# Joint stage with the sums by src four steps ahead and four-step loops, bonds ahead of rows in the sort, and a count of dst ids by comparisons in groups of twelve

## The reference

```python
# layer 0
feat_in  = x @ W_in.T + b_in;  feat_out = x @ W_out.T + b_out
a_in  = seg_mean(feat_in[src],  dst, N)      # edges grouped by dst
a_out = seg_mean(feat_out[dst], src, N)      # edges grouped by src
x = layernorm(x + gru(concat(a_in, a_out), x))
# layer 1
m = relu(concat(x[src], x[dst], bond) @ W1 + b1) @ W2 + b2
m = m * sigmoid(bond @ Wa + ba)
x = layernorm(x + (x + segment_sum(m, src, N)))
```

## Time and profile before

| | |
|---|---|
| median of three runs | 13780.42 us (13775.32 to 13793.6) |
| profiled execution | 13790.1 us, its span 13788.4 us |
| count of dst ids (`load_constants_and_count`) | 0 to 125 us |
| tables and id lists | 125 to 232 us |
| `sum_in_first` | 232 to 2343 us |
| `sort_records` | 2343 to 6660 us |
| joint stage (`sum_rest`) | 6661 to 8841 us |
| node update, messages, finish | 8841 to 13788 us |
| busy shares of the span | PE 63%, DVE 61%, ACT 20%, POOL 70% |

### The profile page before, as it was taken

How to read it: one execution, slowest core, us unless ns; L and a number is a source line. 1 busy time by engine, 2 the same in 40 slices (tenths; PEclk the granted TensorE clock), 3 DMA queues, 4 the chain that set the end, 5 groups by cost and what they waited for, 6 DMA issues and landing times. The chain is left out here.

```text
span 13788.4 us, 248865 instructions
## 1 busy us (share of the span) xinstructions
PE 8650.6 (63%) x53687; PEld 7661.1 (56%) x53688; DVE 8351.6 (61%) x29389; ACT 2713.3 (20%) x7251; POOL 9705.6 (70%) x10125
## 2 busy tenths in 40 slices
PE   3777776333333333333577777797888888888876
PEld 2555554333333333333577777556777777777775
DVE  6555555666666666666677777554444455444444
ACT  0000000111111111111000000154444444444444
POOL 3777776777777777777777777306777777777774
PEclk9555555555656555666788888898999999999998
DMA  5822223666666666666677777513333334333336
GB/s 178 308 54 54 54 54 84 197 198 196 199 196 199 197 199 196 199 196 199 174 187 186 186 186 186 95 52 76 80 79 79 80 88 94 80 79 80 79 79 82
DMA packets 2665496, 1884.08 MB, mean 137 GB/s; under 512 B 1375795, under 2 KB 2460371, under 8 KB 2664784
## 3 DMA queue, kind: packets, MB, share of 16 engines
q1 hardware_dynamic: 1505269, 806.75, 22.1%
q0 software_dynamic: 377360, 782.89, 19.9%
q10 hardware_dynamic: 782662, 292.60, 8.8%
HBM read 1509.53 MB, written 483.44 MB: 145 GB/s over the span
## 5 line engine op out<-in xcount | busy, mean ns | idle before, releaser
L1846 POOL DMA_INDIRECT p<-q_rows,small x3432 | 3250.1, 947 | 1643.5 <-issue 1000.0
L1051 PE MATMUL bank<-p,ring 128*128 x6656 | 1549.0, 426 | 2714.7 <-DVE ring L972 2711.5
L1051 PEld LDWEIGHTS bank<-p,ring 128*128 128x128 f32 x6656 | 1437.8, 328 | 2826.1 <-issue 2826.1
L1110 POOL DMA_INDIRECT edges_a<-ring,small x1664 | 1635.7, 983 | 563.1 <-issue 441.4
L1110 POOL DMA_INDIRECT edges_b<-ring,small x1664 | 1632.5, 981 | 507.6 <-issue 441.1
L799 POOL DMA_INDIRECT ring<-in_x,ring x1664 | 1573.9, 946 | 533.7 <-issue 530.0
L1884 PE MATMUL bank<-ring 128*128 128x256 f32 x3432 | 1205.4, 437 | 766.4 <-DVE p L1796 766.1
L830 PE MATMUL bank<-ring 128*128 128x129 f32 x3328 | 1240.3, 491 | 617.8 <-DMA ring<-in_x,ring 525.1
L1252 POOL DMA_INDIRECT ring<-in_x,small x1352 | 1278.7, 946 | 463.2 <-issue 411.3
L1272 PE MATMUL bank<-p,ring 128*128 128x129 f32 x8360 | 1194.3, 312 | 525.1 <-DVE ring L1200 525.1
L1272 PEld LDWEIGHTS bank<-p,ring 128*128 128x128 f32 x8360 | 1157.7, 226 | 562.5 <-issue 562.5
(11 more groups left out here) (289 smaller groups left out, 14195.4 us busy)
## 6 DMA issues: line engine op xcount, KB each, us to landing
p<-rows_by_slot SPq DMA_DIRECT2D x418, 928.0 KB
p<-edges_b SPq DMA_DIRECT2D x530, 262.0 KB
p<-edges_a SPq DMA_DIRECT2D x520, 262.0 KB
bonds_by_dst<-in_bond ACTq DMA_DIRECT2D x5, 20625.0 KB, 159.1
ring<-edges_a ACTq DMA_DIRECT2D x1792, 33.0 KB
p<-q_rows,small POOLq DMA_INDIRECT x3432
ring<-edges_b ACTq DMA_DIRECT2D x1664, 33.0 KB
ring<-bonds_by_dst ACTq DMA_DIRECT2D x1672, 32.0 KB
```

The lines of the kernel that those rows point to most:

```text
L1051: last = nc.tensor.matmul(found[q][:, j, :], hot_t[g % GRPS][:, QUAD * h + j, :], x, start=True, stop=True, skip_group_check=True)
L1110: pool.indirect_dma_start(out=c.edges[s], out_offset=bass.IndirectOffsetOnAxis(ap=pos[:, k:k + 1], axis=0), in_=rec[:, k, :], in_offset=No ...
L1846: pool.indirect_dma_start(out=gath[g][:, k, :], out_offset=None, in_=c.q_dram, in_offset=bass.IndirectOffsetOnAxis(ap=gidx[g][:, k:k + 1], ...
```

## The change

**Joint stage.** `ids` is split into two transfers: `load_ids` brings the gather indices alone, `load_locals` (new, ring of four) the local numbers. SyncE's pass v becomes: windows of v; wait until `s_hot_in` (counts of `prepare_in`, started at 3) is at least v; locals of v; wait for the last gather of step v-3; ids of v+5. The work by src runs four steps ahead of that by dst: VectorE's turn u is `add_in(u)`, `add_out(u+4)`, `prepare_out(u+6)` in halves, `prepare_in(u+2)`, and TensorE's is `sum_in(u)`, `sum_out(u+5)`; before the loops VectorE does `add_out` and `prepare_out` of four steps, and TensorE `sum_out` of five. The block numbers are read in two register loads, eight before `add_in` and five before `add_out`. The loops of VectorE and TensorE hold four steps instead of eight; the last two loop turns (eight steps) are written out without loop, and leave out what lies past the last step. `sum_out` is zeroed by ScalarE instead of VectorE, which waits for it before its first `add_out`; GpSimd waits for no zeroing.

**Sort.** In SyncE's loop the wait for scatters and the load of bonds stand ahead of the wait for comparisons and the load of rows.

**Count.** Two shifts over all 3300 ids on VectorE, two copies to bf16 on ScalarE, ahead of its weight loads; then five batches of 660 ids. Each batch is 13 + 8 comparisons of 660 bf16 digits with a constant, one for each digit value, into one-hots laid out in groups of twelve ids (group, digit, id); TensorE sums 55 products a batch, now 96 x 156 outputs. The order check is one comparison, written as bf16, ahead of the batches, and its sum is made by ten products with ones on TensorE. Everything is written out without loop.

```diff
-HC, CG = 110, 5
+HC, CG = 660, 12
...
 # ScalarE, ahead of its weight loads
+            for k in range(2):
+                act.wait_ge(s_digit, k + 1)
+                nc.scalar.copy(digits[k], whole[k]).then_inc(s_cast, 1)
...
+            nc.vector.tensor_scalar(whole[0], raw[:, 1, 0:TT], 10, None, ALU.logical_shift_right).then_inc(s_digit, 1)
+            nc.vector.tensor_scalar(whole[1], raw[:, 1, 0:TT], 7, 7, ALU.logical_shift_right,
+                                    ALU.bitwise_and).then_inc(s_digit, 1)
...
-            with dve.Fori(0, HSTEPS // 2) as i:
-                step.loop(i, 4)
-                for n in range(2):
-                    ids = raw[:, 1, bass.ds((2 * i + n) * HC, HC)]
-                    dve.wait_ge(s_cnt, 2 * i + n)
-                    step.mark(nc.vector.tensor_scalar(digits[0], ids, 10, None, ALU.logical_shift_right))
-                    step.link(nc.vector.tensor_scalar(digits[1], ids, 7, 7, ALU.logical_shift_right, ALU.bitwise_and))
-                    for dig, hot, width in ((digits[0], us[n], HU), (digits[1], vs[n], HV)):
-                        nc.vector.tensor_tensor(
-                            hot, dig.unsqueeze(2).to_broadcast([TP, HC, width]),
-                            c.iota[0:TP, 0:width].unsqueeze(1).to_broadcast([TP, HC, width]),
-                            ALU.is_equal).then_inc(s_dig, 1)
...
+            nc.vector.tensor_tensor(after, raw[:, 1, 0:TT], raw[:, 1, 1:TT + 1], ALU.is_gt).then_inc(s_viol, 1)
+            dve.wait_ge(s_cast, 2)
+            for i in range(HSTEPS):
+                n = i % 2
+                if i >= 2:
+                    dve.wait_ge(s_cnt, i - 1)
+                for dig, hot, width in ((digits[0], us[n], HU), (digits[1], vs[n], HV)):
+                    for d in range(width):
+                        nc.vector.tensor_scalar(hot[:, :, d, :], dig[:, i * HC:(i + 1) * HC].rearrange("p (g t) -> p g t", t=CG),
+                                                float(d), None, ALU.is_equal).then_inc(s_dig, 1)
...
-            step.link(nc.vector.tensor_tensor(after[:, 0:TT], raw[:, 1, 0:TT], raw[:, 1, 1:TT + 1], ALU.is_gt))
-            nc.vector.reduce_sum(viol, after[:, 0:TT], AXX).then_inc(s_viol, 1)
...
 # TensorE
+            for i in range(HSTEPS):
+                n = i % 2
+                pe.wait_ge(s_dig, (HU + HV) * (i + 1))
+                for t in range(APART):
+                    last = nc.tensor.matmul(cross, vs[n][:, t, :, :].rearrange("p d t -> p (d t)"),
+                                            us[n][:, t, :, :].rearrange("p d t -> p (d t)"),
+                                            start=(i == 0 and t == 0), stop=(i == HSTEPS - 1 and t == APART - 1))
+                last.then_inc(s_cnt, 1)
+            pe.wait_ge(s_viol, 1)
+            for t in range(0, TT, HC // 2):
+                last = nc.tensor.matmul(c.bank[2][0:1, 0:HC // 2], c.ones[0:TP, 0:1], after[:, t:t + HC // 2],
+                                        start=(t == 0), stop=(t == TT - HC // 2))
...
 # sort_records, SyncE
+                        sp.wait_ge(s_sc[2 * (g % GRPS)], i * (2 * QUAD * 16) + g // GRPS * (QUAD * 16))
+                        load_bonds(u, 2 * (g % GRPS))
                         sp.wait_ge(s_hot, u * 4 + 12)
                         load_rows(u + 2, g % 2)
-                        sp.wait_ge(s_sc[2 * (g % GRPS)], i * (2 * QUAD * 16) + g // GRPS * (QUAD * 16))
-                        load_bonds(u, 2 * (g % GRPS))
...
 # sum_rest, SyncE
+            def load_locals(u, n):
+                sp.dma_start(local[n], c.slots_d[:, bass.ds(u + B_GROUP, 1), LOCAL * HALF:(LOCAL + 1) * HALF]
+                             .rearrange("p o w -> p (o w)")).then_inc(s_loc[n], 16)
...
-                        u = i * LOOK + g
-                        load_windows(u, g % 2, edges)
-                        sp.wait_ge(s_agg_in, u * NI + (IN_0 - (LOOK - AHEAD - 1) * NI))
-                        load_ids(u + AHEAD, (g + AHEAD) % LOOK)
-            for k in range(2):
-                load_windows(QSTEPS + k, k, c.edges[1])
+                        v, last = i * LOOK + g, (g - 3) % GRPS * HALF + HALF - 1
+                        load_windows(v, g % 2, edges)
+                        sp.wait_ge(s_hot_in, v)
+                        load_locals(v, g % TURN_V)
+                        sp.wait_ge(s_g[last], i * (16 * LOOK // GRPS) + 16 * ((g - 3) // GRPS + 1))
+                        load_ids(v + AHEAD, (g + AHEAD) % LOOK)
...
 # VectorE; HOT_0 = 3, LEAD = TURN_V = 4
+            dve.sem_inc(s_hot_in, HOT_0)
-            nc.vector.memset(c.sum_out, 0.0).then_inc(s_zero, 1)
...
+            def turn(i, g, most=QSTEPS):
+                u = i * TURN_V + g
+                add_in(u, blocks_in(u))
+                if g + LEAD < most:
+                    add_out(u + LEAD, g, blocks_out(u + LEAD))
+                for h in range(NO):
+                    if g + LEAD + 2 < most:
+                        prepare_out(i, (g + LEAD + 2) % TURN_V, h, (g + LEAD + 2) // TURN_V)
+                if g + 2 < most:
+                    prepare_in(i, (g + 2) % TURN_V, (g + 2) // TURN_V)
...
+            dve.wait_ge(s_blank, 1)
+            for v in range(LEAD):
+                add_out(v, v, blocks_out(v))
+                for h in range(NO):
+                    prepare_out(0, (v + 2) % TURN_V, h, (v + 2) // TURN_V)
+            with dve.Fori(0, TURNS_S - 2) as i:
+                step.loop(i, TURN_V * NO)
+                for g in range(TURN_V):
+                    turn(i, g)
...
+            nc.scalar.activation(c.sum_out.rearrange("p b d -> p (b d)"),
+                                 c.ones_f[:, 0:1].to_broadcast([P, (NB + 1) * W]), ACT.Copy, scale=0.0).then_inc(s_blank, 1)
...
-            sum_out(0, 0)
-            with pe.Fori(0, QSTEPS // LOOK) as i:
-                for g in range(LOOK):
 # TensorE
+            for v in range(LEAD + 1):
+                sum_out(v, v)
+            with pe.Fori(0, TURNS_S - 2) as i:
+                for g in range(TURN_V):
                     sum_in(i, g)
-                    sum_out(i * LOOK + (g + 1), (g + 1) % LOOK)
+                    sum_out(i * TURN_V + (g + LEAD + 1), g + LEAD + 1)
```

More of the change, by code:

```diff
@@ L226, in load_constants_and_count @@
     pairs = c.pairs()
-    after = scratch[:, 7000:7000 + TT // 2].bitcast(BF16)
-    digits = [scratch[:, 9000 + 200 * n:9000 + 200 * n + HC].bitcast(I32) for n in range(2)]
-    us = [scratch[:, 9600 + 750 * n:9600 + 750 * n + HC * HU // 2].bitcast(BF16).rearrange("p (t d) -> p t d", d=HU)
-          for n in range(2)]
-    vs = [scratch[:, 11200 + 500 * n:11200 + 500 * n + HC * HV // 2].bitcast(BF16).rearrange("p (t d) -> p t d", d=HV)
-          for n in range(2)]
+    after = c.blk_s[0:TP, 0:TT]
+    digits = [scratch[:, 6610 + k * (TT // 2):6610 + (k + 1) * (TT // 2)].bitcast(BF16) for k in range(2)]
+    top = 6610 + TT
+    whole = [scratch[:, top + k * TT:top + (k + 1) * TT].bitcast(I32) for k in range(2)]
+    us = [scratch[:, top + n * (HC * HU // 2):top + (n + 1) * (HC * HU // 2)].bitcast(BF16)
+          .rearrange("p (g d t) -> p g d t", d=HU, t=CG) for n in range(2)]
+    vs = [at.bitcast(BF16).rearrange("p (g d t) -> p g d t", d=HV, t=CG)
+          for at in (c.part(7200, HC * HV // 2)[0:TP, :], c.tab[0:TP, 0:HC * HV // 2])]
+    assert top + HC * HU <= (NB + 1) * XW and 7200 + HC * HV // 2 <= RINGW and HC * HV // 2 <= S_COLS
     spare = 2 * TT
@@ L326, in _ @@
-            step.end(HSTEPS // 2)
+            dve.wait_ge(s_edge, 16)
+            nc.vector.tensor_tensor(after, raw[:, 1, 0:TT], raw[:, 1, 1:TT + 1], ALU.is_gt).then_inc(s_viol, 1)
[8 more added lines that the diff above has]
+                                                float(d), None, ALU.is_equal).then_inc(s_dig, 1)
@@ L340, in _ @@
         def _(pe):
-            pe.sem_inc(s_cnt, 1)
             pe.wait_ge(s_z, 8)
-            nc.tensor.matmul(cross, zero16[:, 0:1].to_broadcast([TP, CG * HU]),
-                             zero16[:, 0:1].to_broadcast([TP, CG * HV]), start=True, stop=False)
-            with pe.Fori(0, HSTEPS // 2) as i:
-                for n in range(2):
-                    pe.wait_ge(s_dig, 4 * i + 2 * n + 2)
-                    for t in range(0, HC, CG):
-                        last = nc.tensor.matmul(cross, us[n][:, t:t + CG, :].rearrange("p t d -> p (t d)"),
-                                                vs[n][:, t:t + CG, :].rearrange("p t d -> p (t d)"),
-                                                start=False, stop=False)
-                    last.then_inc(s_cnt, 1)
@@ L1141, in sum_rest @@
     lo_out = c.small[:, 24:24 + QPS * QW]
-    ids = [c.small[:, 128 + n * 2 * HALF:128 + (n + 1) * 2 * HALF].rearrange("p (f k) -> p f k", k=HALF) for n in range(LOOK)]
+    ids = [c.small[:, 128 + n * HALF:128 + (n + 1) * HALF] for n in range(LOOK)]
+    local = [c.small[:, 256 + n * HALF:256 + (n + 1) * HALF] for n in range(TURN_V)]
     out_bank = [c.bank[0:2], c.bank[2:4]]
@@ L1225, in _ @@
```

(26 more changed lines are left out.)

80 lines of the change are left out of this document (46 added, 34 removed).

## The result

| | before | after |
|---|---|---|
| median | 13777.87 us | 14198.05 us |
| ratio, with its 95% interval | | 1.0303 (1.0283 to 1.0324) |
| span of the profiled execution | 13788.4 us | 14198.7 us |

The account below looks back on a forecast made before the run. VectorE and GpSimd were taken to bound the joint stage together, VectorE by a hair; 582 - 53 - 8 = +521 us on the profiled 13790 us gave 14311, as a median 14300 us, range 14140 to 14520.

Parts of the forecast that it names:

- The term that decides: Joint stage: SyncE's wait for prepare_in holds the next windows, turns of 13.2 us, +582 us.
- The head: Joint stage's start: four steps of src sums ahead of the first add_in, 25 us later than now.
- The last six turns: Joint stage's end: six turns without windows, two each of 7.5, 4.7 and 3.5, 31 us.
- the slow end: Joint stage's last steps, gathering one padded row over and over: 20 us, against 29.7 us now.
- What was said to be hidden: Joint stage: second register load, loop standstill and earlier zeroing (10.7 us) change nothing, covered by the cycle or src steps.
- the second register load: Joint stage, VectorE between two adds: 0.7 us a turn, hidden in the cycle; without it 143 us.
- The loops' standstill: Joint stage, VectorE's loop start: four-step loops remove it, between 0 and 78 us, worth nothing in the cycle.
- if the windows were there: Rival, joint stage: the wait does not bind, turns of 10.4 us, 13735 us in all; chance 0.09.
- second load hidden too: Rival, joint stage: no binding wait, second register load hidden, GpSimd's 10.0 us bound it, 13650 us; chance 0.02.
- TensorE's clock: Part of the longer-cycle rival, joint stage: lower clock or colliding window stream, turns of 15 us, 14660 us; chance 0.09.
- The count: Count stage: 105 comparisons at 0.33 us, 35 us, TensorE's batches behind them, end near 72 us: -53 us.
- The sort: Sort's start: bonds issued first, scatter 6.5 us later as now, 2361.1 instead of 2369.1: -8 us.

Follow-up runs that it names:

- e2: The changed kernel with the local numbers' loads and their wait for prepare_in moved from SyncE's queue to ScalarE's: 13791.5 us, 0.9984 of the kernel before.
- e8: The kernel before with one SyncE wait in the joint stage, ahead of the ids' load, turned into a wait for prepare_in: 14215.3 us, 1.0326.
- e4: The changed kernel with SyncE's register load of the next window starts moved ahead of its wait on s_hot_in, in seven of eight steps: 14115.8 us.
- e3: The changed kernel with VectorE's second register load (five block numbers) put ahead of add_in: 14239.5 us, 1.0308 of its own kernel before.
- e5: The changed kernel with the edits of e2 and e3 together: 13708.9 us, 0.9925 of the kernel before.
- e6: e2 with VectorE's loop holding eight steps again instead of four: 13850.1 us, 1.0060 of the kernel before.
- e1: The changed kernel with the whole joint stage of the kernel before put back: 13741.1 us, 0.9979 of the kernel before.
- e7: e5 with the count in groups of ten ids instead of twelve, 66 groups a batch: 13647.7 us, 0.9912 of the kernel before.

## Why the prediction was right

**The term that decides** was right in mechanism and in place, and a little too long. By its steps (A is VectorE's first add of a turn):
- First window load at A + 2.7: measured 2.62. VectorE there at A + 6.1: measured 6.15.
- First half of the windows 4.9 to 6.2 us after the first issue, taken near the upper end: measured 5.66. This is the term that was mis-sized.
- From the subtraction to the next first add 1.87 + 2.47 = 4.34: measured 4.35.
- Turn 12.4 to 13.4, taken as 13.2: measured 12.67 at the median; from the first add_in (6643.72) to the first turn without windows (9223.91) 2580 us, 12.8 a turn with the slow ones at both ends, where the forecast had 2663. These are 83 of the 102 us by which the stage came out shorter than forecast, 2660 instead of 2762.
- The head: first add_in 47.5 us after the stage's start by the forecast, 48.2 by the trace. The last six turns 31 us by both. The last two turns with windows stand 6.0 and 4.1 us where 2.1 is usual, so the slow end costs some 6 us, not 20.

What shows the cause, beyond the agreement: SyncE waits for prepare_in 6.6 us a turn, the wait taken from its queue (e2) takes 444 us off the stage, the wait alone put into the kernel before (e8) adds 440, and the way made 1.14 us shorter (e4) makes each turn shorter by 0.8.

**What was said to be hidden** was hidden: the second register load costs 0.79 us where it shows (0.7 forecast; in the trace each of VectorE's two loads, of eight and of five values, takes 0.60 us), and taking it away brings nothing in the circle (e3) and 84 us in the stage outside of it (e5 against e2; the forecast's 143 counted no bound by GpSimd). The loops' standstill was worth nothing here, as said: in e8, which has both the wait and the standstill, the turn that ends in the standstill takes 14.7 us and the next one 9.8, together what two others take. Where VectorE bounds, the shorter loop is worth 92 us (e6), more than the 78 that the forecast had as its upper bound.

**The rivals.** The forecast's 10.4 us a turn "if the windows were there" is e2's 10.44, and its "second load hidden too", 10.0 us and 13650, is e5: 10.0 us, and 105 us below the kernel before. Both describe the kernel without the wait, which the change is not. TensorE's clock did fall, to a mean granted clock of 0.78 from 0.88, and its 40 window passes, 4.7 us at the median in the kernel before, take 6.9 here, but with 7.7 us at the most they stay far from the turn's length, and the queue of SyncE does not wait for them.

**The count** ended at 72.4 us where 72 was forecast, by errors that cancel. The comparisons came at 0.405 us and not 0.33, so 42.5 us and not 35. TensorE, sized at 0.13 to 0.15 us a product of 252 columns and as the bound, took 0.07 to 0.11 and bounded nothing. So VectorE was too fast in the forecast, TensorE too slow, and the end the same by luck. The step that failed is the extrapolation from 104 and 128 numbers to 660: it assumed the rate of another shape. The Trainium skill, "VectorE: DVE Perf Modes", section "What auto-detection actually checks", which spoke against the full rate because 55 groups are neither even nor equal to one run of 660, was right, and the 0.48 us worked out beside it is the 0.489 us that one comparison takes; successive comparisons overlap by 0.08, so 105 of them take 42.5 us and not the 50 worked out there. In the trace the source's pattern is one run of 660 and the result's 55 rows of 12. With 66 and 44 groups the rate is there. The trace agrees with the rule.

**The sort** came out 8.6 us shorter, where 8 were forecast, but not step by step. The first scatter, at 2306.79, is 20.5 us after the stage's start instead of 26.5: 6.0 us sooner and not 8. The bonds went out 7.5 us sooner; from them to the scatter it was 8.0 us, where the forecast kept the 6.5 of before. Where the other 2.6 us come from is open. On one chip the stage took 4315.3 us in the old order (e8) and 4305.1 to 4307.1 in the new one (e1, e6, e7). That it is the reordering and not the earlier start was not tried by itself.

**What was not foreseen**: that unchanged stages change. In e1 the untouched joint stage is 18 us longer. The changed kernel's node update is 3.5 us longer too, which is within the 466 to 475 us that this stage takes over all runs.

## What to carry to other kernels

A wait is paid by everything behind it in its queue: before putting a transfer whose place comes free late ahead of one that is needed soon, write down for each what releases it and who needs it next, and add up the legs of the circle (release to issue, issue to landing, landing to release); if the sum is above the engines' own step, that is the new step. Here the queue of an idle engine was the remedy (e2). When a change of several parts is slower, look for the one line before dropping it all: here the count gives 52 us and the sort 8, and the joint stage, with this wait on another queue and the register load moved, 51 more, and the one wait hid them all.

## What the runs showed of the hardware

- A loop of VectorE with a body of 451 instructions, those of its sequencer counted, stands still each time it starts over, 3 us on average and 4.5 at most; with one of 236 it does not. How much is lost in the loop depends on where the code lies: 16 memsets ahead left eight steps at 81.1 us, 48 made them 81.8, and the changed count 81.9.
- A comparison of 660 bf16 numbers with a constant, written in groups, takes 0.489 us with 55 groups of 12, 0.323 with 66 of 10, and 0.364 with 44 of 15; from start to start 0.405, 0.242 and 0.242.
- Five windows of 512 records issued together have their first three in SBUF 5.66 us after the first issue, and 5.97 when they are issued 1.1 us sooner in the turn (e4), beside the same gathers.
